# Two heads per instruction in the attention's products, a logarithm and an exponential in place of the square root, and one output buffer in place of two

## The reference, cut to what matters

```python
x = x + layernorm(L0_attn(layernorm(x)))   # state space layer
x = x + layernorm(L0_ffn(layernorm(x)))    # ternary weights, conv of width 3, silu
x = x + layernorm(L1_attn(layernorm(x)))   # the sublayer that is changed
x = x + layernorm(L1_ffn(layernorm(x)))    # low rank, gelu

def bitlinear(x, w):                       # of L1_attn
    xq = act_quant(rmsnorm(x))             # 1/sqrt(mean(x*x) + 1e-6), then 8 bit
    return einsum('bsd,ed->bse', xq, weight_quant(w))

# L1_attn, with D = 1024, H = 16 heads of Dh = 64
scores = einsum('bshd,bstd->bsht', q, k) / 8    # heads against heads of ONE token
attn = softmax(scores, -1)                      # 16 x 16 for each token
ctx = einsum('bsht,bstd->bshd', attn, v)
ctx = swapaxes(ctx, 1, 2).reshape(B, S, D)
return bitlinear(ctx, wo)
```

## Time and profile before

| what | value |
|---|---|
| median of 3 runs | 11448.71 us (11448.26 to 11455.53) |
| the profiled execution, own time | 11441.06 us |
| its span, slowest core (core 7) | 11439.5 us |
| spans of the eight cores | 11415.2 to 11439.5 us |
| stage b, its two sweeps | about 5147 to 10249 us of the span |
| busy in the whole span, DVE / PE / POOL / ACT | 54% / 23% / 22% / 11% |

### The profile page before, as it was taken

How to read it: one execution, slowest core, us unless ns; L and a number is a source line. 1 busy time by engine, 2 the same in 40 slices (tenths; PEclk the granted TensorE clock), 3 DMA queues, 4 the chain that set the end, 5 groups by cost and what they waited for, 6 DMA issues and landing times.

```text
span 11439.5 us, 73934 instructions; the slowest of 8 cores (11415.2 to 11439.5 us)
## 1 busy us (share of the span) xinstructions
PE 2655.9 (23%) x9842; PEld 1066.2 (9%) x9842; DVE 6179.2 (54%) x11095; ACT 1211.3 (11%) x1667; POOL 2548.6 (22%) x1126
## 2 busy tenths in 40 slices
PE   2321243332033222211111111111111122224444
PEld 1110111111011000100000000000000001101111
DVE  5565677776766777744444444444444445543443
ACT  1110121121000000000000000000000011112222
POOL 0000000000000000005666556665666520000000
PEclk7665687776566666665555555555555556656666
DMA  1014111113211000040000000000000011120000
GB/s 62 34 37 123 39 30 37 30 25 77 82 52 36 31 30 30 30 134 10 11 4 11 6 11 11 4 13 4 11 4 11 6 30 54 54 66 36 30 31 29
DMA packets 191361, 390.74 MB, mean 34 GB/s; under 512 B 72771, under 2 KB 111683, under 8 KB 190662
## 3 DMA queue, kind: packets, MB, share of 16 engines
q1 hardware_dynamic: 161094, 268.56, 7.7%
q0 software_dynamic: 29824, 117.45, 3.7%
HBM read 268.54 MB, written 117.44 MB: 34 GB/s over the span
## 4 chain that ended last, share of the span: by engine, by line
DVE 40%; POOL 22%; PE 14%; issue 11%; ACT 5%; DMA 5%; DVEq 2%; POOLq 0%; ACTq 0%; SPq 0%
POOL b_prodB L1180 12%; POOL b_prodA L1152 9%; PE c_psO L972 4%; PE b_psS L1138 3%; DVEq L66 2%; DVE c_cvscr L789 2%; DVE c_cvscr L792 2%; DVE rndA L931 2%; DVE c_xq L940 2%; DVE rndA L937 2%; DVE rndB L935 2%; DVE c_cbuf L776 2%; DVE c_mx L893 2%; PE b_psS L1277 1%; PE f_psH L538 1%
## 5 line engine op out<-in xcount | busy, mean ns | idle before, releaser
L1180 POOL TENSOR_TENSOR b_prodB<-b_attn,b_vtok 128x1024 bf16<-128x1024 bf16 x512 | 1397.9, 2730 | 319.2 <-DVE b_attn L1173 187.9
L1152 POOL TENSOR_TENSOR b_prodA<-b_qtok,b_ktok 128x1024 bf16<-128x1024 bf16 x512 | 1078.7, 2107 | 1445.6 <-ACT b_ktok L1144 1314.0
L1158 DVE TENSOR_REDUCE b_sc<-b_prodA 128x16 f32<-128x1024 bf16 x512 | 624.7, 1220 | 961.1 <-POOL b_prodA L1152 961.1
L1186 DVE TENSOR_REDUCE b_ctxs<-b_prodB 128x64 f32<-128x1024 bf16 x512 | 624.5, 1220 | 954.5 <-POOL b_prodB L1180 954.5
L1124 PE MATMUL b_psC<-b_identf,b_xn 128*128 128x128 f32 x256 | 103.0, 446 | 3522.2 <-DVE b_xn L1115 3495.2
L972 PE MATMUL c_psO<-c_wtern,c_xq 128*128 128x512 bf16 x2048 | 461.4, 390 | 963.8 <-DVE c_xq L940 963.8
L770 PE MATMUL c_psH<-c_xqT,c_wtern 128*128 128x512 bf16 x2048 | 525.1, 404 | 397.5 <-DVE c_cbuf L776 393.1
L82 POOL DMA_DIRECT2D x<-c_out x8 | 6.0, 746 | 2153.4 <-DVE c_out L996 1911.6
L82 POOL DMA_DIRECT2D c_h<-c_h2st x32 | 28.1, 887 | 1798.7 <-ACT c_h2st L799 1381.1
L1124 PEld LDWEIGHTS b_psC<-b_identf,b_xn 128*128 128x128 f32 x256 | 46.6, 182 | 3579.1 <-issue 3577.4
L972 PEld LDWEIGHTS c_psO<-c_wtern,c_xq 128*128 128x128 bf16 x2048 | 204.9, 100 | 1229.0 <-issue 999.6
(11 more groups left out here) (287 smaller groups left out, 7725.8 us busy)
## 6 DMA issues: line engine op xcount, KB each, us to landing
...
c_h<-c_h2st POOLq DMA_DIRECT2D x16, 1024.0 KB, 24.3
```

Source lines behind the costliest of these rows:

```text
L1152: t_m = p.do("gpsimd", lambda E, h=h: E.tensor_tensor(prodA[:, h % 2, :, :], qtok[:, h, :].unsqueeze(1).broadcast_to([128, 16, 64]), ktok[ ...
L1158: t_s = p.do("vector", lambda E, h=h: E.reduce_sum(scb[:, h, :], prodA[:, h % 2, :, :], axis=AX.X), after=[t_m])
L1180: t_m = p.do("gpsimd", lambda E, h=h: E.tensor_tensor(prodB[:, h % 2, :, :], attnb[:, h, :].unsqueeze(1).broadcast_to([128, 64, 16]), vvie ...
L1186: t_c = p.do("vector", lambda E, h=h, s_i=s_i: E.reduce_sum(ctxs[:, s_i % 2, 64 * h:64 * (h + 1)], prodB[:, h % 2, :, :], axis=AX.X), afte ...
```

## The change

It has three parts.

1. The multiplies on POOL and the sums on DVE take two heads in one instruction instead of one: 8 pairs instead of 16 in each of the two phases, with 2048 products per token in place of 1024. `b_prodA` and `b_prodB` grow to twice their size, and still hold the products of two instructions.
2. With `expln=True`, `ln_stats` and `rms_stats` compute one over the square root as exp(-0.5 * ln(x)): two activations on ACT (Ln, then Exp) in place of the square root on ACT and the reciprocal on DVE. All four calls in stage b set it; the calls in stages a, c and f don't.
3. Sweep 2 has one buffer `b_out` in place of two. The first write to it in a block (L1282) waits for the store of the block before; before the change it waited for the store two blocks earlier.

```diff
--- before.py
+++ after.py
@@ -145,7 +145,7 @@
             after=[t0])
 
 
-def ln_stats(p, x_ap, sq_scr, stat, c0, eps, tok_in=(), n=1024.0):
+def ln_stats(p, x_ap, sq_scr, stat, c0, eps, tok_in=(), n=1024.0, expln=False):
     su, sq, rs, nb = (stat[:, c0 + i:c0 + i + 1] for i in range(4))
     p.do("vector", lambda E: E.reduce_sum(su, x_ap, axis=AX.X), after=tok_in)
     p.do("vector", lambda E: E.scalar_tensor_tensor(
@@ -155,17 +155,28 @@
     p.do("vector", lambda E: E.scalar_tensor_tensor(rs, su, 1.0, su, ALU.mult, ALU.mult))
     p.do("vector", lambda E: E.tensor_sub(sq, sq, rs))
     t7 = p.do("vector", lambda E: E.tensor_scalar_add(sq, sq, eps))
-    t8 = p.do("scalar", lambda E: E.activation(rs, sq, AF.Sqrt), after=[t7])
-    p.do("vector", lambda E: E.reciprocal(rs, rs), after=[t8])
-    t10 = p.do("vector", lambda E: E.scalar_tensor_tensor(nb, su, -1.0, rs, ALU.mult, ALU.mult))
+    if expln:
+        t8 = p.do("scalar", lambda E: E.activation(rs, sq, AF.Ln), after=[t7])
+        t9 = p.do("scalar", lambda E: E.activation(rs, rs, AF.Exp, scale=-0.5), after=[t8])
+        t10 = p.do("vector", lambda E: E.scalar_tensor_tensor(
+            nb, su, -1.0, rs, ALU.mult, ALU.mult), hard=[t9])
+    else:
+        t8 = p.do("scalar", lambda E: E.activation(rs, sq, AF.Sqrt), after=[t7])
+        p.do("vector", lambda E: E.reciprocal(rs, rs), after=[t8])
+        t10 = p.do("vector", lambda E: E.scalar_tensor_tensor(
+            nb, su, -1.0, rs, ALU.mult, ALU.mult))
     return rs, nb, t10
 
 
-def rms_stats(p, x_ap, sq_scr, stat, c0, eps, tok_in=(), n=1024.0):
+def rms_stats(p, x_ap, sq_scr, stat, c0, eps, tok_in=(), n=1024.0, expln=False):
     sq, rs = stat[:, c0:c0 + 1], stat[:, c0 + 1:c0 + 2]
     p.do("vector", lambda E: E.scalar_tensor_tensor(
         sq_scr, x_ap, 1.0, x_ap, ALU.mult, ALU.mult, accum_out=sq), after=tok_in)
     t2 = p.do("vector", lambda E: E.tensor_scalar(sq, sq, 1.0 / n, eps, ALU.mult, ALU.add))
+    if expln:
+        t3 = p.do("scalar", lambda E: E.activation(rs, sq, AF.Ln), after=[t2])
+        t4 = p.do("scalar", lambda E: E.activation(rs, rs, AF.Exp, scale=-0.5), after=[t3])
+        return rs, t4
     t3 = p.do("scalar", lambda E: E.activation(rs, sq, AF.Sqrt), after=[t2])
     t4 = p.do("vector", lambda E: E.reciprocal(rs, rs), after=[t3])
     return rs, t4
@@ -1049,8 +1060,8 @@
     qtok = sb(stk, nc, "b_qtok", [128, 16, 64], BF16)
     ktok = sb(stk, nc, "b_ktok", [128, 16, 64], BF16)
     vtok = sb(stk, nc, "b_vtok", [128, 16, 64], BF16)
-    prodA = sb(stk, nc, "b_prodA", [128, 2, 16, 64], BF16)
-    prodB = sb(stk, nc, "b_prodB", [128, 2, 64, 16], BF16)
+    prodA = sb(stk, nc, "b_prodA", [128, 2, 2, 16, 64], BF16)
+    prodB = sb(stk, nc, "b_prodB", [128, 2, 2, 64, 16], BF16)
     scb = sb(stk, nc, "b_sc", [128, 16, 16], F32)
     attnb = sb(stk, nc, "b_attn", [128, 16, 16], BF16)
     smx = sb(stk, nc, "b_smx", [128, 16], F32)
@@ -1077,13 +1088,13 @@
         t_q = None
         for s_i in range(NST):
             xs = xsb[:, s_i, :]
-            rs, nb, tst = ln_stats(p, xs, sq_scr[:], sta, 12 * s_i, 1e-5,
+            rs, nb, tst = ln_stats(p, xs, sq_scr[:], sta, 12 * s_i, 1e-5, expln=True,
                                    tok_in=[t_load[k], L.get("b_stat%d_%d" % (bi, s_i))])
             t_xn = p.do("scalar", lambda E, xs=xs, rs=rs, nb=nb: E.activation(
                 xn_f[:], xs, AF.Identity, bias=nb, scale=rs),
                 after=[t_load[k], L.get("b_xnw")], hard=[tst])
             rs2, trs2 = rms_stats(p, xn_f[:], sq_scr[:], sta, 12 * s_i + 4,
-                                  1e-6, tok_in=[t_xn])
+                                  1e-6, tok_in=[t_xn], expln=True)
             t_xr = p.do("scalar", lambda E, rs2=rs2: E.activation(
                 sq_scr[:], xn_f[:], AF.Identity, scale=rs2),
                 after=[L.get("b_sqw")], hard=[trs2])
@@ -1148,16 +1159,18 @@
                     L["war_b_psS%d" % half] = t_pr[(nm, half)]
             L["b_xqTw"] = mm
             t_sc = []
-            for h in range(16):
-                t_m = p.do("gpsimd", lambda E, h=h: E.tensor_tensor(
-                    prodA[:, h % 2, :, :],
-                    qtok[:, h, :].unsqueeze(1).broadcast_to([128, 16, 64]),
-                    ktok[:], ALU.mult),
-                    after=[t_pr[("q", h // 8)], t_pr[("k", 0)], t_pr[("k", 1)],
-                           L.get("b_prA%d" % (h % 2))])
-                t_s = p.do("vector", lambda E, h=h: E.reduce_sum(
-                    scb[:, h, :], prodA[:, h % 2, :, :], axis=AX.X), after=[t_m])
-                L["b_prA%d" % (h % 2)] = t_s
+            for hg in range(8):
+                t_m = p.do("gpsimd", lambda E, hg=hg: E.tensor_tensor(
+                    prodA[:, hg % 2, :, :, :],
+                    qtok[:, 2 * hg:2 * (hg + 1), :].unsqueeze(2)
+                        .broadcast_to([128, 2, 16, 64]),
+                    ktok[:].unsqueeze(1).broadcast_to([128, 2, 16, 64]), ALU.mult),
+                    after=[t_pr[("q", 0)], t_pr[("q", 1)], t_pr[("k", 0)],
+                           t_pr[("k", 1)], L.get("b_prA%d" % (hg % 2))])
+                t_s = p.do("vector", lambda E, hg=hg: E.reduce_sum(
+                    scb[:, 2 * hg:2 * (hg + 1), :], prodA[:, hg % 2, :, :, :],
+                    axis=AX.X), after=[t_m])
+                L["b_prA%d" % (hg % 2)] = t_s
                 t_sc.append(t_s)
             t_mx = p.do("vector", lambda E: E.reduce_max(
                 smx[:], scb[:], axis=AX.X), after=t_sc)
@@ -1176,18 +1189,20 @@
             L["b_scw"] = t_at
             vview = vtok[:].transpose([0, 2, 1])
             t_cx = []
-            for h in range(16):
-                t_m = p.do("gpsimd", lambda E, h=h: E.tensor_tensor(
-                    prodB[:, h % 2, :, :],
-                    attnb[:, h, :].unsqueeze(1).broadcast_to([128, 64, 16]),
-                    vview, ALU.mult),
+            for hg in range(8):
+                t_m = p.do("gpsimd", lambda E, hg=hg: E.tensor_tensor(
+                    prodB[:, hg % 2, :, :, :],
+                    attnb[:, 2 * hg:2 * (hg + 1), :].unsqueeze(2)
+                        .broadcast_to([128, 2, 64, 16]),
+                    vview.unsqueeze(1).broadcast_to([128, 2, 64, 16]), ALU.mult),
                     after=[t_at, t_pr[("v", 0)], t_pr[("v", 1)],
-                           L.get("b_prB%d" % (h % 2))])
-                t_c = p.do("vector", lambda E, h=h, s_i=s_i: E.reduce_sum(
-                    ctxs[:, s_i % 2, 64 * h:64 * (h + 1)], prodB[:, h % 2, :, :],
-                    axis=AX.X),
+                           L.get("b_prB%d" % (hg % 2))])
+                t_c = p.do("vector", lambda E, hg=hg, s_i=s_i: E.reduce_sum(
+                    ctxs[:, s_i % 2, 128 * hg:128 * (hg + 1)].rearrange(
+                        "p (a b) -> p a b", b=64),
+                    prodB[:, hg % 2, :, :, :], axis=AX.X),
                     after=[t_m, L.get("b_ctxs%d" % (s_i % 2))])
-                L["b_prB%d" % (h % 2)] = t_c
+                L["b_prB%d" % (hg % 2)] = t_c
                 t_cx.append(t_c)
             g = NST * k + s_i
             t_cw = p.dma("gpsimd", ctx_dram[128 * g:128 * (g + 1), :],
@@ -1204,7 +1219,8 @@
     ctxl = sb(stk, nc, "b_ctxl", [128, 1024], F32)
     ctxq_f = sb(stk, nc, "b_cq", [128, 1024], F32)
     ctxqT = sb(stk, nc, "b_cqT", [128, 8, 128], BF16)
-    out_sb = [sb(stk, nc, "b_out%d" % i, [128, NST, 1024], F32) for i in range(2)]
+    out_sb1 = sb(stk, nc, "b_out", [128, NST, 1024], F32)
+    out_sb = [out_sb1, out_sb1]
 
     x2_t = [None] * NSS
 
@@ -1225,7 +1241,7 @@
                          after=[L.get("b_ctxl"),
                                 ("dc0", p.cnt["dc0"]), ("dc1", p.cnt["dc1"])])
             rs2, trs2 = rms_stats(p, ctxl[:], sq_scr[:], sta, 12 * s_i, 1e-6,
-                                  tok_in=[t_cl])
+                                  tok_in=[t_cl], expln=True)
             t_xr = p.do("scalar", lambda E, rs2=rs2: E.activation(
                 sq_scr[:], ctxl[:], AF.Identity, scale=rs2),
                 after=[t_cl, L.get("b_sqw")], hard=[trs2])
@@ -1282,12 +1298,12 @@
                 t_e = p.do("scalar", lambda E, s_i=s_i, half=half, pg=pg, osc=osc: E.activation(
                     osb[:, s_i, 512 * half:512 * (half + 1)], pg[:, 0:512],
                     AF.Identity, scale=osc),
-                    after=[mm, L.get("b_outw%d" % bi)], hard=[t_os])
+                    after=[mm, L.get("b_outw")], hard=[t_os])
                 L["war_b_psS%d" % half] = t_e
                 L["b_cqTw"] = mm
                 t_ep.append(t_e)
             rs3, nb3, tst3 = ln_stats(p, osb[:, s_i, :], sq_scr[:], sta,
-                                      12 * s_i + 7, 1e-5, tok_in=t_ep)
+                                      12 * s_i + 7, 1e-5, tok_in=t_ep, expln=True)
             t_ln = p.do("vector", lambda E, s_i=s_i, rs3=rs3, nb3=nb3, osb=osb: E.tensor_scalar(
```

(4 more changed lines are left out.)

## The result

The changed kernel takes 11207.04 us (median of 8 runs, 11203.18 to 11219.42) against 11448.49 us (8 runs): ratio 0.9791, 95% interval 0.9780 to 0.9802. It is 241 us faster; the forecast was 193 us faster, 11256 us, with its own range from 11135 to 11358.

What follows compares the result with a forecast made beforehand. Bound by its order, a serial chain of tiles in stage b, not by an engine. Terms -123 (two heads), -80 (loads) and +10 (arithmetic) gave -193 us: 11256 us, own range 11135 to 11358, to 11400 for 8 in 10.

Steps and rivals of the forecast that it cites:

- The bound: Stage b: no engine near full, tiles follow serially at 128 us each, so each microsecond saved shortens the span.
- The waits between multiplies: POOL, both phases of sweep 1: 512 waits of 0.274 us fall away, 140 us saved.
- The multiplies themselves: POOL, both phases: 512 fixed shares of 0.10 us saved, 51 us; ends 0 and 147 us.
- The sums: DVE: sums of 2.29 us stay hidden except each phase's last, 1.07 us longer, 64 times: 68 us lost.
- The table loads: ACT, stage b and stage f: 62 fewer loads at 1.29 us, 80 us saved, assuming one set holds Ln and Exp.
- The arithmetic: Layer norm and RMS statistics: Ln and Exp chains 0.09 and 0.07 us longer in 64 tiles, 10 us lost.
- One output buffer: Sweep 2: the store lands 12 us before the new wait, so cost 0; range 0 to 25 us.
- The clock: TensorE's projections in sweep 1: idle before them barely changes, counted 0, with 26 us either way.
- alternating tables: Rival, stage b: Ln and Exp from two sets, 193 more loads, 249 us lost, 11585 us; chance 0.11.
- a third set: Rival, sweep 1: softmax's exponential from another set, two loads a tile stay, -113 us, 11336 us; chance 0.05.
- the costlier multiply: Rival, POOL: two heads cost over twice one, scores up to 319 us more, 11626 us; chance 0.10.
- nothing happens: Rival, POOL's phases: multiplies' waits did not hold the chain, so no gain; excluded by the rows, no chance given.

Runs made afterwards that it cites:

- four edits of POOL's row: Separate runs: last pair as single heads 11171.17 us, four heads an instruction 11215.92, groups shrinking to single heads 11079.32, two heads with one output buffer 11275.41.
- the runs of the parts: Kernel before with only two heads per instruction and one output buffer, 11275.41 us; kernel before with only Ln and Exp in four calls, 11385.30 us.
- a split pair: Changed kernel with the last pair of heads of each phase as two single heads, nine multiplies a phase: 11171.17 us, ratio 0.9758.
- four heads: Changed kernel with four heads in an instruction, four instructions a phase, product tiles twice as large: 11215.92 us, ratio 0.9797.
- part 2 alone: Kernel before with only Ln and Exp in the four calls; one head per instruction and two output buffers stay: 11385.30 us, ratio 0.9944.
- one square root left: Changed kernel with the RMS statistics of sweep 1 back on square root and reciprocal: 11280.17 us, ratio 0.9853.

## Why the prediction was right, and where it was off

**The bound.** Right. Stage b is one serial chain of tiles, and each saved piece came back at its full length: four edits of POOL's row met their sums within 11 us (36 against 39, -9 against -20, 128 against 127, and 173 against 165 for part 1), and the time of a tile fell by 8.0 us. The prediction's sum for part 1 was 123 us and for part 2 it was 70; the runs of the parts gave 173 and 63. So the miss of 48 us lies in part 1.

**The waits between multiplies.** Right: 262.9 us of idle became 122.4, 140 saved.

**The multiplies themselves.** The mechanism was right and the size was off, and this is the largest miss. The term was 512 x 0.10 = 51 us, a choice between two rows of other instructions, nearer to the memset of one column; it measured 256 x (0.181 + 0.183) = 93 us. The bounds of 0 and 0.287 held it. Neither row had the value in it: the memset took 0.098 us in all, and the affine select less 128 columns at 1.9 ns leaves 0.04. The prediction's own sign, multiplies of 4.1 to 4.2 and 5.3 to 5.5 us, was missed for that reason: they take 4.03 and 5.28. So was its tile of about 123 us, which takes 120.5.

The figure of 4497 ns that the Trainium skill ("GPSIMD Engine Reference", section 3.1) has for an fp32 add of this length isn't that of these bf16 products, 4033 ns; the measured figure decides, and the 98 us less that the prediction worked out from 4497 don't show.

**The sums.** Right: 2286 ns where 2.29 us was worked out, and the tail of a phase costs what it lasts, 68 us, which the runs with a split pair and with four heads show from both sides.

**The table loads.** Right: 62 fewer, 1.29 us each, and 80 less the 13 that the projections lost are 67, against the 63 us that part 2 alone gained. A switch of 2.66 us would have given 165. That one set serves Ln and Exp was an assumption; the one load at L159 and the run with one square root left show it.

**The arithmetic.** Off by 10 us: counted at 10 us lost, it measured nothing, 64 x (0.03 - 0.04) = -1 us. The step took ACT's pause behind its own instruction, 0.15 us, from activations of 512 columns; between these small ones it is 0.09 (0.29 us from Ln's start to Exp's, where the prediction gave 0.35 as its sign).

**One output buffer.** Right: no cost, by the run with two and by its sweep 2.

**The clock.** Counted at nothing with 26 us either way. It moved within that: the projections' mean went from 9.14 to 9.00 us, 4 us gained in the whole change, but 10 gained and 13 lost in its parts. That the whole came out near 0 is in part luck.

With the measured terms the sum is -140 - 93 + 68 - 80 - 1 - 4 = -250 us, against 241 and 246 in two groups of runs. On core 7 of the two profiles sweep 1 is shorter by 249.5 us (4121.0 to 3871.5), sweep 2 longer by 1.2, and stage b begins 5 us later; that start differs by 19 us between the cores 0 and 7 of one execution before. So the sum holds for sweep 1, and most of the few us between it and the time arise ahead of stage b, which the change doesn't touch. The 1.2 us of sweep 2 stay open; the single buffer isn't their cause, by the run with two.

Of the rivals, alternating tables and a third set are refuted by the loads, the costlier multiply by 4033 and 5277 ns, and "nothing happens" by the 241 us.
